# First edge stage of a graph network on Trainium2: source columns copied on chip in every third group of edges, register loads ahead of the waits

## What is computed

```python
h = jnp.maximum(_layernorm(x, axis=-1), 0.0)
msg_in = jnp.concatenate([h[src], h[dst], edge_attr], axis=-1)
hid = jax.nn.relu(msg_in @ msg_W1 + msg_b1)
messages = hid @ msg_W2 + msg_b2
aggregated = jax.ops.segment_sum(messages, dst, num_segments=x.shape[0])
u = jax.nn.relu(jnp.concatenate([h, aggregated], axis=-1) @ upd_W1 + upd_b1)
x = x + _layernorm_affine(h + u @ upd_W2 + upd_b2)
```

## Time and profile before

| | us |
|---|---|
| median of 3 runs | 3791.6 |
| lowest and highest | 3791.53, 3792.68 |
| the profiled execution's own time | 3790.61 |
| its span, first to last instruction | 3788.8 |
| of it, gathers of the first edge stage | from 48.2 to 1895 |
| of it, gathers of the second edge stage | from 1913 on |

### The profile page before, as it was taken

How to read it: one execution, slowest core, us unless ns; L and a number is a source line. 1 busy time by engine, 2 the same in 40 slices (tenths; PEclk the granted TensorE clock), 3 DMA queues, 4 the chain that set the end, 5 groups by cost and what they waited for, 6 DMA issues and landing times.

```text
span 3788.8 us, 90744 instructions
## 1 busy us (share of the span) xinstructions
PE 2952.5 (78%) x19656; PEld 2513.2 (66%) x19786; DVE 3118.5 (82%) x20049; ACT 2821.3 (74%) x17211; POOL 2822.8 (75%) x2992
## 2 busy tenths in 40 slices
PE   6788888888888788788867777777777777777776
PEld 5787877778877778787845555555555555555554
DVE  5677777777777777777659999999999999999997
ACT  4666666666666666666548888888888888888884
POOL 6777777777777777777767777777777777777775
PEclk8878787878787887878779999999999999999999
DMA  7455555555555555555443333333333333333332
GB/s 201 135 142 142 143 142 140 149 144 142 140 144 140 145 142 141 143 141 143 112 118 89 90 91 90 90 90 90 91 91 90 91 91 90 90 90 90 90 91 57
DMA packets 364600, 442.62 MB, mean 117 GB/s; under 512 B 174981, under 2 KB 221411, under 8 KB 364047
## 3 DMA queue, kind: packets, MB, share of 16 engines
q1 hardware_dynamic: 269535, 243.82, 22.3%
q0 software_dynamic: 94112, 192.73, 20.4%
q10 hardware_dynamic: 400, 0.20, 0.0%
HBM read 413.17 MB, written 23.28 MB: 115 GB/s over the span
## 4 chain that ended last, share of the span: by engine, by line
POOL 67%; issue 22%; PE 4%; DMA 4%; DVE 2%; ACT 1%; SPq 0%; DVEq 0%; ACTq 0%; POOLq 0%
POOL t_ring L1028 37%; POOL m_ring L1016 30%; DMA m_ring<-tab_a,src_t 3%; PE bank L1688 1%; PE bank L1664 1%; DVE m_pre L1771 1%; PE bank L1675 1%; DMA tab_a<-m_pre 0%; DVE lone L977 0%; PE bank L1693 0%; ACT m_hid L1719 0%; ACT lone L1731 0%; DMA t_ring<-tab_l,src_t 0%; PE bank L2445 0%; PE bank L1324 0%
## 5 line engine op out<-in xcount | busy, mean ns | idle before, releaser
L1028 POOL DMA_INDIRECT t_ring<-tab_l,src_t x1472 | 1399.1, 950 | 466.4 <-issue 447.6
L1016 POOL DMA_INDIRECT m_ring<-tab_a,src_t x1469 | 1399.5, 953 | 459.3 <-issue 446.8
L2529 ACT ACTIVATE lone<-X 128x4 uint8 x7360 | 740.0, 189 | 68.7 <-issue 63.2
L1688 PE MATMUL bank<-w,m_attr_t 128*128 128x128 f32 x3128 | 697.1, 350 | 6.9 <-ACT m_attr_t L1728 6.5
L1731 ACT ACTIVATE lone<-HT 128x4 uint8 x6080 | 621.4, 190 | 74.5 <-issue 60.5
L1664 PE MATMUL bank<-m_hot,m_hid 128*128 128x32 f32 x3128 | 482.2, 302 | 236.6 <-ACT m_hid L1719 230.8
L1664 PEld LDWEIGHTS bank<-m_hot,m_hid 128*128 128x128 f32 x3128 | 451.0, 222 | 289.7 <-ACT m_hid L1719 283.0
L1688 PEld LDWEIGHTS bank<-w,m_attr_t 128*128 128x128 f32 x3128 | 603.9, 240 | 48.2 <-DVE m_hot L1756 13.5
L1771 DVE TENSOR_TENSOR m_pre<-bank,m_ring 128x512 f32<-128x512 f32 (+1 forms) x391 | 255.9, 654 | 415.9 <-DMA m_ring<-tab_a,src_t 320.9
L1719 ACT ACTIVATE m_hid<-m_pre 128x512 f32<-128x512 f32 x391 | 246.0, 629 | 416.8 <-DVE m_pre L1771 366.2
L977 DVE COPY lone<-HT 128x4 uint8 x6080 | 496.4, 195 | 61.2 <-issue 58.5
(11 more groups left out here) (268 smaller groups left out, 5984.6 us busy)
## 6 DMA issues: line engine op xcount, KB each, us to landing
m_ring<-in_edge_attr_dram SPq DMA_DIRECT2D x390, 256.0 KB
t_rows<-dst_rows SPq DMA_DIRECT2D x196, 256.0 KB
m_rows<-dst_rows SPq DMA_DIRECT2D x196, 192.0 KB
t_ring<-tab_l,src_t POOLq DMA_INDIRECT x1472
m_ring<-tab_a,src_t POOLq DMA_INDIRECT x1469
m_win<-tab_b SPq DMA_DIRECT2D x391, 24.0 KB
t_win<-tab_r SPq DMA_DIRECT2D x391, 24.0 KB
tab_b<-n_b SPq DMA_DIRECT2D x47, 96.0 KB
```

The costliest lines, as they stand in the source:

```text
L1016: pool.indirect_dma_start(out=r.got[u][0:rows, j, :], out_offset=None, in_=k.tab_a, in_offset=bass.IndirectOffsetOnAxis(ap=k.src_t[0:rows, ...
L1028: pool.indirect_dma_start(out=r.got[u][0:rows, j, :], out_offset=None, in_=k.tab_l, in_offset=bass.IndirectOffsetOnAxis(ap=k.src_t[0:rows, ...
L1688: pe.matmul(p_hid[q % 2][:, e], lhsT=attr_t[q % 2][:, e], rhs=k.w1[:, 2, :], start=True, stop=False)
L2529: late_move(k, loaded, lambda out, col: act.activation(out, col, ACT.Copy), s["t_pick_s"])
```

## The change

The picked groups of the first stage become every third one (`V` = 3): 8, 11, ... 389. The 128 columns of a picked group are now copied in the three slots v = g - 4 to g - 2, 44, 44 and 40 columns, of which DVE copies 24, 24 and 20 and ACT 20, 20 and 20 (`COLUMNS`). `pick_columns` is split in two. `pick_load` holds the waits (`m_places`, `m_hp`) and the register load and now stands at the head of the group's work in the slot: on DVE ahead of the wait for the loaded inputs and of the two masks, on ACT ahead of the wait for `m_attrp` and of the copy that follows it. `pick_move` holds the copies and stands where `pick_columns` stood. On ACT `placed` stays between them. SP calls `fetch_picked` in each slot, for the group two on, where it was called for one slot in four. Counts for the semaphores are worked out by `picks_until` from the list of picked groups.

```diff
-V = 4
-PICKED = P // V
-BY_VECTOR = 16
+V = 3
+COLUMNS = {3: ((24, 20), (24, 20), (20, 20))}
+DEPTH = 2
...
+def picks(k):
+
+    return [g for g in range(k.groups) if picked(k, g)]
+
+
+def span(k, g):
+
+    own = picks(k)
+    n = own.index(g)
+    return g - own[n - 1] if n else 3
+
+
+def picks_until(k, g):
+
+    own = picks(k)
+    return g - (own[0] - span(k, own[0])) if g >= own[0] else 0
+
+
+def being_picked(k, v):
+
+    for n, g in enumerate(picks(k)):
+        if 0 <= v + SOONER - (g - span(k, g) + 1) < span(k, g):
+            return n, g, v + SOONER - (g - span(k, g) + 1)
+    return None
+
+
+def placed(act, k, m, v):
+
+    now = being_picked(k, v + 1)
+    if now is None or now[2]:
         return
...
+    n, g, i = now
+    act.wait_ge(m["m_ids"], 16 * (n + 1))
+    if n >= 2:
+        act.wait_ge(m["m_picked_v"], picks_until(k, picks(k)[n - 2]))
+        act.wait_ge(m["m_picked_s"], picks_until(k, picks(k)[n - 2]))
...
+def pick_load(nc, eng, k, m, v, engine):
+
+    now = being_picked(k, v)
+    if now is None:
+        return None
+    n, g, i = now
+    if i == 0:
+        if n == 0:
+            eng.wait_ge(k.s_ht, k.n_ht)
+        eng.wait_ge(m["m_places"], n + 1)
+        if n >= DEPTH:
+            eng.wait_ge(m["m_hp"], picks(k)[n - DEPTH] + 1)
+    columns = COLUMNS[span(k, g)]
+    first = sum(a + b for a, b in columns[:i]) + engine * columns[i][0]
+    _, places = nc.values_load_multi_w_load_instructions(
+        k.places[n % 2][:, first:first + columns[i][engine]], engines=[eng.engine], min_val=k.ht_at,
...
+def pick_move(k, loaded, move, done):
+
+    if loaded is None:
         return
...
+    n, first, places = loaded
+    for q, place in enumerate(places):
+        last = move(k.lone[:, n % DEPTH, first + q:first + q + 1].bitcast(U8),
+                    k.HT[:].bitcast(U8)[:, bass.ds(place - k.ht_at, 4)])
     last.then_inc(done, 1)
...
-                    if u % V == 2:
-                        fetch_picked(sp, k, s, t["src"], (g + 2) // V)
+                    fetch_picked(sp, k, s, t["src"], g + 2)
...
                         g = rnd * U + u
+                        loaded = pick_load(nc, act, k, s, g, 1)
                         after(act, s["m_attrp"], g + 1)
                         act.activation(attr_t[u % 2][:], p_attr[u % 2][:], ACT.Copy).then_inc(s["m_attr"], 1)
-                        placed(nc, act, k, s, g)
-                        pick_columns(nc, act, k, s, g, BY_VECTOR, PICKED - BY_VECTOR,
-                                     lambda out, col: act.activation(out, col, ACT.Copy), s["m_picked_s"])
+                        placed(act, k, s, g)
+                        pick_move(k, loaded, lambda out, col: act.activation(out, col, ACT.Copy), s["m_picked_s"])
...
                         g = rnd * U + u
+                        loaded = pick_load(nc, dve, k, s, g, 0)
                         hold(dve, r.s_in[u], n_in[u] * (rnd + 1))
...
-                        pick_columns(nc, dve, k, s, g, 0, BY_VECTOR, dve.tensor_copy, s["m_picked_v"])
+                        pick_move(k, loaded, dve.tensor_copy, s["m_picked_v"])
```

More of the change, by code:

```diff
@@ L946, in picked @@
     return g % V == V - 1 and U <= g < k.groups - 1
-def placed(nc, act, k, m, g):
-    n, i = (g + SOONER + 1) // V, (g + SOONER + 1) % V
-    if i or not picked(k, n * V + V - 1):
-        return
[L954 to L957, removed]
+def picks(k):
[4 more added lines that the diff above has]
+    return g - own[n - 1] if n else 3
@@ L958, in placed @@
     act.activation(k.places[n % 2], k.ids[n % 2], ACT.Copy, scale=4.0, bias=float(k.ht_at)
                    ).then_inc(m["m_places"], 1)
-def pick_columns(nc, eng, k, m, g, first, many, move, done):
-    n, i = (g + SOONER) // V, (g + SOONER) % V
-    if not picked(k, n * V + V - 1):
-        return
[L967 to L978, removed]
+def pick_load(nc, eng, k, m, v, engine):
[13 more added lines that the diff above has]
+        k.places[n % 2][:, first:first + columns[i][engine]], engines=[eng.engine], min_val=k.ht_at,
+        max_val=k.ht_at + 4 * (k.N - 1),
+        skip_runtime_bounds_check_because="src names rows of the node features, as the gathers take it")
+    return n, first, places
@@ L979, in pick_columns, with fetch_picked @@
+def pick_move(k, loaded, move, done):
+    if loaded is None:
+        return
+    n, first, places = loaded
+    for q, place in enumerate(places):
+        last = move(k.lone[:, n % DEPTH, first + q:first + q + 1].bitcast(U8),
+                    k.HT[:].bitcast(U8)[:, bass.ds(place - k.ht_at, 4)])
     last.then_inc(done, 1)
-def fetch_picked(sp, k, m, src, n):
-    g = n * V + V - 1
+def fetch_picked(sp, k, m, src, g):
     if not picked(k, g):
         return
[L987 to L990, removed]
+    n = picks(k).index(g)
+    if n >= 2:
+        sp.wait_ge(m["m_places"], n - 1)
+    if n:
+        sp.wait_ge(m["m_ids"], 16 * n)
@@ L1603, in body @@
                     sp.wait_ge(k.s_wtc, 1)
-                    fetch_picked(sp, k, s, t["src"], U // V)
+                    for g in range(U, U + 2):
+                        fetch_picked(sp, k, s, t["src"], g)
                     return
@@ L1681, in body @@
                         if picked(k, g):
-                            n = g // V % 2
-                            pe.wait_ge(s["m_picked_v"], g + 1 - U)
-                            pe.wait_ge(s["m_picked_s"], g + 1 - U)
+                            n = picks(k).index(g) % DEPTH
+                            pe.wait_ge(s["m_picked_v"], picks_until(k, g))
+                            pe.wait_ge(s["m_picked_s"], picks_until(k, g))
                         for j in range(J):
```

## The result

| | before | after |
|---|---|---|
| time, median of 4 runs | 3791.95 us | 3844.51 us |
| lowest to highest | 3791.53 to 3792.68 | 3835.52 to 3858.65 |
| profiled execution: own time, span | 3790.6, 3788.8 | 3836.4, 3834.6 |

The account below looks back on a forecast made before the run. GpSimd's back-to-back gathers, 1.256 us each, were taken as the first stage's bound. Removing 33 saves 41.4 us: 3790.6 - 41.4 + 0.5 = 3749.7, with the median 1.0 above, 3750.7 us; range 3745 to 3784.

Parts of the forecast that it names:

- the cover of DVE's load: DVE's load ahead of the masks: work queued before it covers most of 1.52 us, leaving 0.3 us a group bare.
- the second stage's loads: Lower bound for DVE's bare load: nothing, as second-stage loads already stand ahead of the wait with 0.1 us idle before 2292 copies.
- Rival (a): DVE takes the bound, waits before `m_pre` delaying its load: 0.8 us bare, 4.87 us a group, 3853 us; chance 0.15.
- DVE's own work: DVE's group without waits or bare load: 3.53 us now plus 0.54 for more column copies, 4.07 us.
- Loads as worked out: DVE's register loads at 0.063 us a register: 1.60 us for 24 registers, 1.35 for 20.
- The wait for places: DVE's wait for `m_places`, now in front of the masks: taken as 0.1 us a group, bounds nothing to 0.6.
- ACT: ACT's group: 3.17 + 0.43 for copies and place row + 0.4 bare load = 4.00 us, under 4.61.
- PE: PE's group: two 306 ns matmuls for a third of the groups, +0.05, so 3.99 us; it fits.
- 1436 gathers: First edge stage on GpSimd: 33 of 1469 gathers go, leaving 1436, each about 1.256 us behind the last.
- four groups ahead: GpSimd's waits on older groups would hold it only if it were four groups further ahead.
- The end: End of the first stage: last copies two slots later, DVE may lag a little more, +0.5 us.
- Rival (c): Port rule scales: more DVE copies raise a gather's extra cost from 7 to 10 ns, 4 us less gain, 3755 us; chance 0.04.

Follow-up runs that it names:

- e10: Changed kernel with DVE's waits and load ahead of the masks only in the four slots behind a chain, behind the masks elsewhere: 3826.69 us, ratio 1.0098.
- e9: Changed kernel with DVE's waits and load ahead of the masks only in the four slots without a chain before them, behind the masks elsewhere: 3769.32 us, ratio 0.9943.
- e7: Changed kernel, same order and full loads, but DVE makes only one column copy per slot, the others left out: 3747.06 us, ratio 0.9878.
- e4: Changed kernel with only the waits ahead; register loads back behind the masks (DVE) and the attribute copy (ACT): 3788.11 us, ratio 0.9992.
- e5: Changed kernel with DVE's waits and load back behind the masks, ACT's still ahead: 3774.15 us, ratio 0.9953.
- e3: Changed kernel with DVE's waits and load for the next slot put before the node tile's steps, ACT unchanged: 3770.55 us, ratio 0.9944.
- e1: Changed kernel with waits and loads of both engines back behind the masks (DVE) and the attribute copy (ACT): 3778.23 us, ratio 0.9955.
- e6: e3 with DVE's copies of a slot split into two halves, the reduce of the masks between them: 3792.15 us, ratio 0.9994.
- e12: e3 with 16 columns a slot on DVE and 28, 28, 24 on ACT: 3799.56 us, ratio 1.0026.
- e11: e3 with 20 columns a slot on DVE and 24, 24, 20 on ACT: 3756.63 us, ratio 0.9909.
- e8: e3 with ACT's load also moved behind the attribute copy: 3780.03 us, ratio 0.9958.

## Why the prediction was wrong, step by step

**The step that failed is the cover of DVE's load**: "A slot with more node work covers more ... and leaves 0.2", and from it "I take 0.3". The bare load measured 0.72 us a group. It was worked out from the busy time in front of the masks, as if DVE's sequencer were always as far ahead as the queue is long. Of the two slots that I read the earlier trace rows, one had no chain in front: its load started at 836.68, before `m_pre`. The other, the one with more node work, did: its load started at 834.27, 0.09 us after the chain's last step, and was covered only as the two masks stood behind that step. Ahead of the masks, which start at 834.46, all but 0.2 us of it would have been bare. So a slot with a chain covers less, though it has more node work, the reverse of the step. A row that hinted at it was in hand: the copies at 835.42 have 0.35 us bare before them, those at 838.42 none, though both have the same two masks in front. The trace of before shows what stood between, and the code which of it waits (the tile's steps before the two slots):

```profile
834.00 0.15 DVE L1451 RECIPROCAL n_rs<-n_sd 128x1 f32<-128x1 f32 x1
834.18 0.16 DVE L1453 SCALAR_TENSOR_TENSOR n_nm<-n_mv,n_rs 128x1 f32<-128x1 f32 x1
...
837.63 0.28 DVE L1399 TENSOR_TENSOR n_tiles<-n_tiles,n_b 128x128 f32<-128x128 f32 x1
```

The second of these waits for the first; the last waits for neither. I saw the gap and didn't ask why the one slot had it. That the second stage's loads stand ahead of the wait and cost nothing bounded nothing here, as no run showed chains before them.

**Rival (a) had the number by luck.** It said 0.8 bare and 4.87 us a group; 0.72 and 4.88 came (4.86 over 100 to 1850 us). It blamed the waits in front of `m_pre`; these cost 0.19 us a group now, and e10 against e9 has the same waits with 57 us between them. Its argument against itself, that a late DVE doesn't stop at those waits and gets covered again, is where the forecast leaned; the runs show it in the slots without a chain alone (0.22 us bare a slot there in e9, 1.24 behind a chain in e10). The rival's time, 3853, is 8.5 us over the median. Its mechanism is real all the same where DVE does wait: e7's slots without a chain have 0.74 us bare, its "0.7", and with the chains 1.0 us a group. That also tells against the forecast as it stood: a DVE under the pace, which is what it needs, doesn't have 0.3 bare but 1.0, and 4.07 + 1.0 is over 4.61.

**The other terms.** DVE's own work, 3.53 + 0.54 = 4.07, measured 4.88 - 0.72 - 0.19 = 3.97, as a copy took 360.7/4624 = 0.078 us and not 0.082. Loads as worked out: 1.60 for 24 registers and 1.35 for 20. The wait for places, 0.1: e4 puts the waits at 10 us in all, 0.03 us a group, in the range. ACT: 719.2/205 = 3.51 busy and 108.4/204 = 0.53 bare, 4.04 against 4.00 without its waits, and harmless (e5). PE: 862.7/205 = 4.21 us against 3.99, at a granted clock of 0.77 where it was 0.81; in e3 4.08 at 0.79, still not the bound. 1436 gathers: right. GpSimd was to be held only from four groups ahead: it got there, and was held, which is why the ends moved as they did. The end, "+0.5 us": 18.8 us, since a DVE that is the bound leaves its lag behind.

**What the gain lost besides: the gathers got dearer.** Where the forecast's premise is restored (e3: GpSimd hardly held), 41.4 us were to come and the profiled span is 26.8 shorter (3762.0); that execution is e3's fastest, and by the medians it is 21.3. The page's lines of e3 and of after for the stage's gathers:

```profile
L1055 POOL DMA_INDIRECT m_ring<-tab_a,src_t x1436 | 1383.6, 963 | 450.2 <-issue 423.3
```

```profile
L1055 POOL DMA_INDIRECT m_ring<-tab_a,src_t x1436 | 1378.7, 960 | 505.3 <-issue 398.3
```

Before, the mean over the stage was 953 ns. 10 ns more on 1436 gathers are 14.4 us, and 41.4 - 14.4 = 27.0: for the profiled execution the sum closes. Rival (c) had copies that hold gathers and scaled them with their number from 7 ns, which gave 4 us; but those 7 ns aren't the copies', as e7 has 951 ns with one copy a slot. It goes with unbroken runs. GpSimd and DVE of e1:

```profile
469.60 2.31 POOL L1055 DMA_INDIRECT m_ring<-tab_a,src_t  x1 [0.30 <-issue]
```

```profile
470.00 1.79 DVE L1016 COPY lone<-HT 128x4 uint8 x24
471.70 0.36 DVE L1806 TENSOR_REDUCE m_hot_n<-m_hot 128x32 bf16<-128x128 f32 x1
```

A gather that takes 0.94 us otherwise lasts until 471.91, past the end of the run of 24 copies that began during it. With one copy the longest gather between 100 and 1850 us is 1.17 us (e7), with runs of 12 1.39 (e6), with 16 1.32 in the kernel before and 1.58 in e12, with 20 1.51 (e11), with 24 1.79 to 2.45 (e9, after). Such gathers are few, 23 of 1436 over 1.3 us in e3, and most of them come at one place of the run. In e3:

```profile
301.84 1.80 POOL L1055 DMA_INDIRECT m_ring<-tab_a,src_t  x1 [0.30 <-issue]
```

```profile
301.16 1.79 DVE L1016 COPY lone<-HT 128x4 uint8 x24
```

Counted over the traces, a gather that starts 0.67 to 0.69 us into a run mostly lasts as long as the run: 19 of 23 in e3 (1.79 us with 24 copies, 1.5 with 20), 19 of 22 in e11 (1.5 with 20), 19 of 24 in e12 (1.22 with 16), but 3 of 11 in the kernel before and 9 of 23 in e1. Of the 495 of e3 that start elsewhere in a run, 3 last over 1.1 us. So the run's length sets how long such a hold is, and how the gathers fall against the runs how many there are. At that one place, runs of 16 held 19 gathers in e12 and 3 before. Not all of it is the copies': the changed kernel has a gather of 1.37 us at 722.50, and DVE copies no columns between 721.59 and 724.17. The Trainium skill, SBUF — State Buffer, section "SBUF: two separate sides", says that a DVE copy with two ports locks GpSimd out of the shared pair for as long as the instruction lasts, so that no descriptors are written; the copy that it names for this is one of fp32. The trace agrees that copies hold gathers, here of uint8; a single copy of 0.19 us can't hold one for 0.85 (1.79 - 0.94) or for 1.37 us (e1), and here it was the whole run.

**Left open.** Why a gather is held at that one place of a run, what holds those outside of it (ten of e12's last 1.3 to 1.6 us and begin before the run), why e6's loads start later, and the spread of e3, e5, e8 and e9 within some 10 us. That the hold is the port pair is argued, and no run takes another cause away.

## What to carry to other kernels

Ahead of a register load, count as cover only what the sequencer can pass without stopping: steps that wait for each other through semaphores cover no more than the last of them, however long they are. Put the load in front of such a chain, not behind it, and move it only on an engine with time to spare. When work is taken off GpSimd and put on VectorE as small copies, keep the share no larger than the pace needs, and expect unbroken runs to hold gathers: 20 columns beat 24 (ratios 0.9909 and 0.9944), 16 moved the bound to ScalarE and TensorE, and splitting the runs made the gathers cheaper but the kernel slower (e6).

## What the runs showed of the hardware that I had not expected

- A register load on DVE starts 0.01 to 0.09 us after the last instruction of a chain of waits has started (1001.24 and 1001.32; all 103 such loads of the changed kernel, 600 to 1600 us), though that instruction is still running; in slots without a chain it starts earlier and is covered up to 0.22 us ahead of the masks (e9) and 0.04 behind them (e10), as long as DVE doesn't wait for other engines (0.74 in e7). The Trainium skill, Perfetto Trace Analysis, section "Sequencer Loop", says that a sequencer hands engine instructions on and goes to the next one, while control instructions run in the sequencer itself. The trace agrees where nothing waits (the load at 836.68 of before, with `m_pre` still to start at 836.90); what the waits of a chain do to it is this case's rows.
- A gather can last 2.31 us (e1) and up to 2.45 us (after) instead of 0.94 when a run of 24 copies of 4 bytes falls against it, and one that starts 0.67 to 0.69 us into a run mostly lasts as long as the run (1.22, 1.5, 1.79 us for 16, 20, 24 copies); mean over the stage 951 ns with one copy (e7), 953 with runs of 16 (before), 963 with 24 (e3).
- A copy of 4 bytes alone takes 0.191 us (e7), an unbroken run of 24 of them 1.79, of 20 1.51 and of 16 1.22 us: 0.12 us a run and 0.07 a copy, an estimate from these. The fixed part overlaps with what follows (the reduce at 302.87 in e3 starts before the run's end at 302.95), and splitting the runs cost DVE no busy time (e6).
